# Two windowed attention layers: values with the tokens on the partitions, sums from a column of ones, and x normalised on ScalarE

## The reference

```
x = x + L0(gn(x))   # attention in 4 windows of 8x8 tokens, 12 heads of 8 channels, a bias per head
x = x + L1(gn(x))   # the same windows on the image rolled by 4, 12 heads of 32 channels, masks, a shared bias
x = x + L2(gn(x))   # depthwise 3x3 and pointwise convolution, quantised weights
x = x + L3(gn(x))   # linear attention with rounding
```

```
attn = softmax(q @ k.T * scale + bias)   # 64 x 64
out  = attn @ v                          # 64 x 8 (L0) or 64 x 32 (L1)
y    = concat(out over the heads) @ w_out + b
```

## Time and profile before

| | us |
|---|---|
| median of 3 runs | 624.99 |
| lowest, highest | 619.41, 633.68 |
| profiled execution, its own time | 622.26 |
| its span, first to last instruction | 620.5 |
| mean granted TensorE clock in it, share of full speed | 0.936 |
| busy: PE, VectorE, ScalarE, GpSimd | 448.3, 480.5, 236.2, 192.9 |

### The profile page before, as it was taken

The page is one execution under the profiler, slowest core; times in us unless marked ns, Lnnn a source line. Parts: engine busy times, 40 slices in busy tenths (PEclk is TensorE's granted clock), DMA queues, the critical chain, the costliest instruction groups (busy, mean ns, idle before and its releaser), DMA issues.

```text
span 620.5 us, 14087 instructions
## 1 busy us (share of the span) xinstructions
PE 448.3 (72%) x4973; PEld 291.5 (47%) x4973; DVE 480.5 (77%) x931; ACT 236.2 (38%) x538; POOL 192.9 (31%) x302
## 2 busy tenths in 40 slices
PE   0285787878787776877777777777776668856674
PEld 0284555656565554555555555555554322223342
DVE  0855798888888765788888888888887469957784
ACT  0001444444453333344444444444432123235763
POOL 6020444434343422322222222222233114330312
PEclk9999999999998788899999999999999789977887
DMA  9300000000000000000000000000000000000011
GB/s 278 53 2 0 3 3 2 0 0 0 0 0 0 1 1 1 2 1 1 1 0 0 0 0 0 0 0 0 0 1 2 1 0 1 0 2 13 13 39 39
DMA packets 8511, 7.08 MB, mean 11 GB/s; under 512 B 5058, under 2 KB 8130, under 8 KB 8354
## 3 DMA queue, kind: packets, MB, share of 16 engines
q1 hardware_dynamic: 3984, 5.26, 2.9%
q10 hardware_dynamic: 4498, 1.44, 1.3%
HBM read 5.13 MB, written 1.57 MB: 11 GB/s over the span
## 4 chain that ended last, share of the span: by engine, by line
PE 49%; DVE 32%; issue 8%; ACT 6%; DMA 2%; POOL 1%; DVEq 1%; ACTq 1%; POOLq 0%
DVE inv_sum L942 13%; PE bank L757 9%; PE bank L727 9%; PE bank L766 6%; PE bank L779 5%; PE bank L816 4%; DVE conv L1177 4%; PE bank L784 3%; PE bank L1258 3%; PE bank L794 3%; DVE v L885 3%; DVE probs L927 2%; DMA table<-in_L_conv_rpb_table 2%; PE bank L560 2%; PE bank L800 2%
## 5 line engine op out<-in xcount | busy, mean ns | idle before, releaser
L967 POOL TENSOR_TENSOR probs<-probs,row_max 128x384 f32<-128x384 f32 x128 | 106.5, 832 | 292.7 <-DVE row_max L929 292.7
L942 DVE RECIPROCAL inv_sum<-bank 128x384 f32<-128x384 f32 (+1 forms) x48 | 109.8, 2287 | 30.2 <-PE bank L784 21.8
L825 ACT ACTIVATE probsT<-bank 128x384 f32<-128x384 f32 x128 | 62.8, 491 | 158.5 <-PE bank L766 158.3
L927 DVE TENSOR_TENSOR probs<-bank,bias 128x384 f32<-128x384 f32 x128 | 70.4, 550 | 39.0 <-PE bank L757 37.9
L929 DVE TENSOR_REDUCE row_max<-probs 128x6 f32<-128x384 f32 x128 | 70.8, 553 | 4.4
L766 PE MATMUL bank<-cst,probs 128*128 128x128 f32 x384 | 71.7, 298 | 0.8 <-ACT probsT L825 0.7
L727 PE MATMUL bank<-xn,w 128*128 128x256 f32 x192 | 51.4, 406 | 26.8 <-ACT k L861 22.5
L757 PE MATMUL bank<-k,q 64*64 64x128 f32 x1536 | 62.0, 295 | 8.8 <-DVE probs L927 5.8
L757 PEld LDWEIGHTS bank<-k,q 64*64 64x64 f32 x1536 | 46.0, 143 | 30.8 <-issue 29.5
L766 PEld LDWEIGHTS bank<-cst,probs 128*128 128x128 f32 x384 | 45.6, 147 | 27.4 <-issue 18.1
L727 PEld LDWEIGHTS bank<-xn,w 128*128 128x128 f32 x192 | 35.0, 195 | 43.6 <-ACT k L861 26.4
(11 more groups left out here) (146 smaller groups left out, 688.1 us busy)
## 6 DMA issues: line engine op xcount, KB each, us to landing
rel_bc<-in_L_conv_rel_index SPq DMA_DIRECT2D x1, 2048.0 KB, 8.9
x<-in_x SPq DMA_DIRECT2D x4, 384.0 KB, 12.1
out_dram<-y_out SPq DMA_DIRECT2D x8, 192.0 KB, 2.1
cst<-in_consts ACTq DMA_DIRECT2D x1, 485.0 KB
w<-in_L_conv_w_qkv ACTq DMA_DIRECT2D x1, 432.0 KB, 4.7
p<-in_L_conv_w_out ACTq DMA_DIRECT2D x1, 144.0 KB, 4.6
pos<-in_L_conv_pos_emb SPq DMA_DIRECT2D x8, 2.0 KB
b_qk<-in_L_conv_qkv_b ACTq DMA_DIRECT2D x8, 0.1 KB, 6.7
```

The costliest lines, as they stand in the source:

```text
L825: nc.scalar.activation(probsT[w][:, :], ps_probsT[:, 0:NP * 128], ACT.Exp).then_inc(L.s.probsT_sb, 1)
L927: nc.vector.tensor_tensor(out, scores, b, ALU.add).then_inc(L.s.biased, 1)
L942: nc.vector.reciprocal(of(inv), of(ps_sums)).then_inc(L.s.inverted, 1)
L967: nc.gpsimd.tensor_tensor(probs[w][:, :, :], probs[w][:, :, :], by_row(row_max[w]), ALU.subtract).then_inc(L.s.shifted, 1)
```

## The change

- `pe_values`: `probsT` is now the stationary operand (64 columns) and v the moving one. v has a column of ones behind the channels of each head, so that a product of 66 columns in L1 (18 in L0) gives values and sums for two heads at once. The tokens lie on the partitions. Products 784 and 800 are gone; there are still 12 products per pair.
- `dve_heads`: the reciprocal of 12 sums per partition (L1, per pair) or 24 (L0, per sample), and one product with it repeated over the channels (128x384 or 128x192), into the new `headsN`.
- `pe_turn` (new): TensorE transposes that back, 3 transposes per pair in L1, 2 per sample in L0; `act_heads` (new) copies it out of PSUM into the buffer that the output product reads.
- `act_norm` in place of `dve_norm`: x is normalised by ScalarE as rstd*x + shift.
- The second v of L1 is copied out by VectorE, no longer by ScalarE.
- The output product `pe_out(s-1)` moves from before scores(s+1,0) to after q (L0) or qk0, qk1 (L1) of s+2; `act_out(s-1)` moves from w = 1 to the end of w = 3, behind the copies there.
- The bias of v is added in `act_heads`, product 552 and its wait are gone: the bias table's products wait for their one-hot input alone. Eight small memsets of ones and a shorter table of constants.

The diff, cut:

```
...
-        v0 = [sb(f"v0_{i}", [128, NW * NP, NU, NU * NH * HD0]) for i in range(2)]
+        v0 = [sb(f"v0_{i}", [128, 2, 2 * NP * NU, NH * (HD0 + 1)]) for i in range(2)]
-        v1 = [sb(f"v1_{i}", [128, NW, NP * NU, NH * HD1]) for i in range(2)]
+        v1 = [sb(f"v1_{i}", [128, NW, NP * NU, NH * (HD1 + 1)]) for i in range(2)]
-        inv_sum = [sb(f"inv_sum{i}", [128, NP * PAIR_COLS]) for i in range(2)]
+        inv_sum = [sb(f"inv_sum{i}", [128, 2 * HEADS]) for i in range(2)]
+        headsN = [sb(f"headsN{i}", [128, INNER]) for i in range(2)]
...
-            dve.wait_ge(pe_prep, PE_BV)
-            step(nc.vector.tensor_tensor(p0_bv[:, :], bank[1][0:C, C:C + 1], p0_b[:, :], ALU.add))
...
-            pe.wait_ge(dve_prep, done["p0T"])
-            nc.tensor.matmul(bank[1][0:C, C:C + 1], p0T[0:C, :], b0_v[:, :], start=True, stop=True).then_inc(pe_prep, 1)
+            pe.wait_ge(dve_prep, done["onehot"])
...
-                        ("v", 0, "dve", 4), ("v", 1, "act", 4)]
+                        ("v", 0, "dve", 4), ("v", 1, "dve", 4)]
...
+            for g in range(NP * NU):
+                p, u = g // NU, g % NU
                 for c in range(2):
...
+                    last = nc.tensor.matmul(ps_heads[c * WT:(c + 1) * WT, at_:at_ + n],
+                                            probsT[2 * j + u][:, p * 128 + c * WT:p * 128 + (c + 1) * WT], v,
+                                            start=True, stop=True)
...
+        def pe_turn(pe, L, s, j):
+
+            pe.wait_ge(L.s.divided, head_count(L, s, j))
+            wait(pe, L.s.heads_sb, heads_before(L, s, j, 1))
+            rows = 128 if L.wide else C
+            for p in range(NP if L.wide else 2):
+                last = nc.tensor.transpose(ps_headsT[0:rows, p * 128:(p + 1) * 128],
+                                           head_buffer(L, s, j)[:, p * rows:(p + 1) * rows], ident)
+            last.then_inc(L.s.turned, 1)
...
+        def act_norm(act, L, s):
...
+            for of_image, of_tokens in window_pieces(L):
+                tokens = xn[parity(s)][0:C, :, :].rearrange("c w t -> c (w t)")
+                nc.scalar.activation(of_tokens(tokens), of_image(image(x_of(s))), ACT.Identity, bias=gn_shift[:, bass.ds(s * 1, 1)],
+                                     scale=gn_rstd[:, bass.ds(s * 1, 1)]).then_inc(L.s.xn_ready, 1)
...
+        def act_heads(act, L, s, j):
+            act.wait_ge(L.s.turned, head_count(L, s, j))
...
+                nc.scalar.copy(heads1[parity(s)][:, :, j * PAIR_COLS:(j + 1) * PAIR_COLS],
+                               ps_headsT[:, 0:NP * PAIR_COLS].rearrange("r (p q) -> r p q", p=NP)).then_inc(L.s.heads_sb, 1)
...
+                nc.scalar.activation(heads0[parity(s)][0:C, :], ps_headsT[0:C, 0:T], ACT.Identity,
+                                     bias=b0_v[:, 0:1]).then_inc(L.s.heads_sb, 1)
...
+            nc.vector.reciprocal(inv, src[:, :, L.hd]).then_inc(L.s.inverted, 1)
+            dve.wait_ge(L.s.inverted, head_count(L, s, j))
+            nc.vector.tensor_tensor(dst, src[:, :, 0:L.hd], inv.unsqueeze(2).broadcast_to([128, groups, L.hd]),
+                                    ALU.mult).then_inc(L.s.divided, 1)
...
                     if q[2]:
                         pe_qkv(pe, L, *q)
-                if j == 0 and prev:
-                    pe_out(pe, L, moved(s, -1))
+                    if w == 2 and prev:
+                        pe_out(pe, L, moved(s, -1))
+                if (j and L.wide) or (not j and prev):
+                    pe_turn(pe, L, *pair_at(s, j - 1))
 
         def act_sample(act, L, s, prev, nxt, nxt2):
             for w in range(NW):
+                if w == 2 and prev:
+                    act_heads(act, L, moved(s, -1), 1)
+                if w == 0 and L.wide and prev:
+                    act_heads(act, L, moved(s, -1), 0)
                 act_exp(act, L, s, w)
                 evacuate_step(act, "act", L, s, w, nxt, nxt2)
-                if w == 1 and prev:
+                if w == 1 and nxt2:
+                    act_norm(act, L, moved(s, 2))
+                if w == 3 and prev:
                     act_out(act, L, moved(s, -1))
...
-                if w == 1 and nxt2:
-                    dve_norm(dve, L, moved(s, 2))
...
+            act_norm(act, L, 0)
             evacuate_first(act, "act", L, 0, 0, L.qk_uses)
+            if before:
+                act_heads(act, before, B - 1, 1)
+            act_norm(act, L, 1)
             if before:
                 act_out(act, before, B - 1)
...
```

More of the change, by code:

```diff
@@ L71, in constants @@
     ch = np.arange(C)
[L72 to L75, removed]
     put("group_mean", (ch[:, None] // GROUP == ch[None] // GROUP) / np.float32(GROUP * T), C)
@@ L156, in build @@
         ps_probsT = bank[2]
-        ps_sums = bank[3]
+        ps_headsT = bank[3]
         ps_heads = bank[4]
@@ L403, in build @@
                         *(t[:, :, :, :] for t in pad)]
+        one_columns = [(t, h, hd) for t, hd in (*((t, HD0) for t in v0), *((t, HD1) for t in v1)) for h in range(NH)]
+        ZEROED = len(zero_buffers) + len(one_columns)
         def pool_prepare(pool):
@@ L408, in pool_prepare @@
                 pool.wait_ge(zeroed, i + 1)
+            for i, (t, h, hd) in enumerate(one_columns):
+                nc.gpsimd.memset(t[h * WT:(h + 1) * WT, :, :, h * (hd + 1) + hd], 1.0).then_inc(zeroed, 1)
         def pool_prepare_late(pool):
@@ L771, in pe_values @@
             pe.wait_ge(L.s.probsT_sb, win_count(s, 2 * j + 1))
-            par = parity(s)
+            par, n = parity(s), NH * (L.hd + 1)
             if L.wide:
                 evacuated(pe, L, s, L.qk_uses + j)
[L775 to L789, removed]
-                for c in range(2):
[L791 to L803, removed]
@@ L806, in pe_out @@
         def pe_out(pe, L, s):
-            pe.wait_ge(L.s.heads_sb, pair_count(s, 1) if L.wide else s + 1)
+            pe.wait_ge(L.s.heads_sb, head_count(L, s, 1))
             wait(pe, L.s.y_ready, s * 1)
@@ L831, in act_out @@
             nc.scalar.activation(y_attn[:, :], ps_mix[0:C, 0:T], ACT.Identity,
-                                 bias=(p1_b if L.wide else p0_bv)[:, 0:1]).then_inc(L.s.y_ready, 1)
+                                 bias=(p1_b if L.wide else p0_b)[:, 0:1]).then_inc(L.s.y_ready, 1)
         def evac_q(eng, L, s, i, j, slot):
@@ L949, in dve_new_x @@
             dve_stats(dve, L.n + 1, s)
-        def dve_norm(dve, L, s):
-            if isinstance(s, int) and s < 2 and L.n:
-                dve.wait_ge(L0.s.v_ready, (B - 1 + s) * L0.v_uses)
-            wait(dve, L.s.v_ready, s * L.v_uses - L.v_uses)
-            for of_image, of_tokens in window_pieces(L):
-                tokens = xn[parity(s)][0:C, :, :].rearrange("c w t -> c (w t)")
-                nc.vector.tensor_scalar(of_tokens(tokens), of_image(image(x_of(s))), gn_mean[:, bass.ds(s * 1, 1)],
-                                        gn_rstd[:, bass.ds(s * 1, 1)], ALU.subtract, ALU.mult).then_inc(L.s.xn_ready, 1)
         def by_row(r):
@@ L1079, in pe_first @@
             if before:
+                pe_turn(pe, before, B - 1, 1)
                 pe_out(pe, before, B - 1)
@@ L1446, in _ @@
             pe_last_values(pe, L1)
+            pe_turn(pe, L1, B - 1, 1)
             pe_out(pe, L1, B - 1)
@@ L1462, in _ @@
             act.wait_ge(late_in, LATE_IN)
-            act.wait_ge(dve_prep, done["p0_bv"])
             act_first(act, L0, None)
@@ L1467, in _ @@
             attention_loop(act, L1, act_sample, None)
+            act_heads(act, L1, B - 1, 0)
+            act_heads(act, L1, B - 1, 1)
             act_out(act, L1, B - 1)
```

61 lines of the change are left out of this document (32 added, 29 removed).

## The result

| | before | after |
|---|---|---|
| median of 4 runs, us | 624.24 | 590.27 |
| lowest, highest | 619.41, 633.68 | 587.53, 594.22 |
| profiled execution, its own time | 622.26 | 589.08 |
| its span | 620.5 | 587.1 |
| granted clock in it, share of full speed | 0.936 | 0.921 |

The ratio is 0.9485 [0.9395, 0.9575]: 5% faster, within 2.3 us of the forecast 588.

A forecast was written before the change was run, and what follows sets the result against it. VectorE and TensorE taking turns in a chain through the reciprocal was taken as the bound. Terms -4.9 - 0.7 - 14.7 - 3.5 - 3 - 9.5 = -36.3 took 622.26 to 586.0, 588 against run medians; range 571 to 608.

The forecast's parts named there:

- L0's loop (term -14.7): L0's period per sample falls from 9.85 to 8.8 us, over 14 samples -14.7 us.
- the GpSimd chain: In L0, y out, residual add, subtraction, second add, statistics and bias step set the period of 8.8 us.
- TensorE's floor: L0's period through TensorE's own loop of multiply and bias step, should GpSimd's path be quicker: 8.1 to 8.3 us.
- rival (d): Granted clock falls where TensorE waits in L1: +73 us there, 660 in all, slower than before; chance 0.04.
- L1's loop (-3): L1's period goes from 15.5 to 15.2 us; over 14 samples -3 us, bounds +7 and -11.
- the gain of the short reciprocal is given to two waits: In each L1 sample TensorE waits twice for 1.6 us, on VectorE's copy of v and ScalarE's of k.
- Seam (-3.5): Between L0 and L1, one shorter chain against the second v and a turn: -3.5 us, bounds -1 and -6.
- end of L1 (-9.5): From scores(15,1) to the first pad, three chains with shorter reciprocal and sums: -9.5 us, bounds -6 and -13.
- Preparation (-4.9 and -0.7): Before L0, bias products start earlier, moving all behind by 4.9 us; first normalisations on ScalarE give 0.7 more.
- the sign to look for: The first q product of L0 starts near 47.9 us, where it was 52.7.
- Rival (b): Loads and products of `pe_values` don't overlap, a pair takes 1.7 us: +24 us, 612 in all; chance 0.06.
- Small terms: Reciprocals of 12 and 24 sums cost 231 and 306 ns; ScalarE's normalisation pieces 0.33 to 0.5 us each.

The follow-up runs named there:

- y_first_L0: The changed kernel with ScalarE in L0 copying the output of s-1 out ahead of the three copies of q: 568.66 us, ratio 0.9188 to the kernel before.
- filler_L0: The changed kernel with six unread products of constants per L0 sample, where TensorE waits ahead of T(s,1): 574.67 us, ratio 0.9185 to the kernel before.
- v1_on_scalar: The changed kernel with the second v of L1 copied out by ScalarE again: 558.07 us, ratio 0.8951 to the kernel before.
- prep_alone: The kernel before with only the preparation changed, bias products waiting only for their one-hot input: 620.36 us, ratio 0.9979 to the kernel before.
- norm_on_vector: The changed kernel with x normalised on VectorE again: 629.63 us, ratio 1.0002 to the kernel before.
- norm_vector_filled: norm_on_vector with eight unread products per L1 sample ahead of qk1, where TensorE waited: 604.17 us, no ratio given.

## Why the prediction was right, and where it was not

- **The total**: 588 forecast, 590.27 measured. Against the profiled spans the sum said -36.3, and -33.4 came. But it came right by errors of opposite sign: L0's loop gave 12 us less than forecast for its 12 samples, and the seam and the end of L1 some 12 more. That these cancel was luck.
- **L0's loop (term -14.7)**: failed. Measured over 12 samples: -0.56. The walk itself held: period 8.8 forecast, 8.40 to 8.94 in the samples at full clock, with the GpSimd chain as the bound, which y_first_L0 took away. TensorE's floor without it was given as 8.1 to 8.3; it is 7.87. What failed was to price the granted clock in L1 alone, as rival (d), and to take L0's 7.3 us of TensorE work in a period of 8.8 at full clock. The walk made two new waits of TensorE there, 1.19 and 0.46 us, and every second sample behind them fell to the lower level, which cost 3 us each time. filler_L0 isolates it. The 9.85 to compare with was too short also: it is one sample, and the mean of the 12 before was 10.06.
- **L1's loop (-3)**: the period at full clock was 15.0 to 15.1 against 15.2 forecast, with the two waits on VectorE's v and on the copy of k, 1.7 and 1.58. Three of the 11 samples took 16.7 behind the wait for v, and the mean is 15.49, as before. (15.2 against 15.5 over 14 samples is -4.2, not the -3 of the sum.) The mechanism of rival (d) is there, with some 5 us in place of its 73.
- **The reading behind L1**: "the gain of the short reciprocal is given to two waits" is right, and v1_on_scalar shows that one line undoes one of them, for 32 us.
- **Seam (-3.5) and end of L1 (-9.5)**: too small. From L0's 13th reciprocal to L1's 4th the gain was 10.1, of which the L0 term had counted two samples, some 2 us. From L1's 26th reciprocal to the first pad it was 18.1 (16.97 and 6.42 to 5.28 us at the last), where the prediction counted from scores(15,1) on and got 9.5 for what measures 11.45. The last samples have no next one to fill them, and their work is a chain as the end is; the prediction gave them the loop's 0.25. And it priced the low clock there, 0.88 and 0.86 before, only for the products of the sums, while the whole stretches rose to 0.96 and 1.00; how much of the gain is which was not tested.
- **Preparation (-4.9 and -0.7)**: -4.66 to the first q product, at 48.08 against 47.9. The two terms add up to 5.6, which would have been 47.1, so the sum and the sign to look for didn't agree. prep_alone gives 3.99 for the first, 0.9 too little; the rest, 0.67, is near the second.
- **`pe_values`**: 0.85 us for 24 records in L1's chain and 0.88 in L0's timeline, forecast 0.85 and 0.8. Rival (b), loads that are not overlapped, isn't there. The Trainium skill's page TensorE: Matmul & The Clock Gate, section LDWEIGHTS (loading the stationary operand), gives a load as columns/1.2 ns; an estimate from it for 24 loads of 64 columns is 1.28 us, and the trace, with 0.85 and 0.88, again disagrees.
- **Small terms**: the reciprocals at 228 and 307 ns, from 156 + 6.24 per element, are exact to 3 ns. ScalarE's pieces came at 0.40 to 0.48 us.
- **What didn't hold on the way**: the gain does not come from where VectorE's busy time fell. norm_on_vector has the short reciprocal too and is no faster than before.

The places where the clock fell are read from one execution of the kernel after. Its other three had a granted clock of 0.907, 0.915 and 0.932 over the whole span where this one has 0.921, so the loss is in all four; in which samples it lay there was not traced.

## What to carry to other kernels

When an edit frees an engine, look at what stands behind each job before giving it new ones: here the same change is worth 5% with the second v copied by VectorE and 10.5% with it copied by ScalarE, because TensorE's next product waited for that copy. Walk a period on one instruction that recurs, and subtract neighbours in the trace: stages that mix a loop and its ends hid that both loops had gained next to nothing. Price the granted clock wherever a walk leaves TensorE a new wait in each period, and if the wait can't go, try products in it whose result nobody reads.

## What the hardware showed that was not expected

- In L0, TensorE's granted clock fell behind two waits of 1.19 and 0.46 us with 1.2 us of work between them, in every second sample. Before, with waits of other lengths, the same stage mostly kept the full clock (0.94), and three of the 12 loop samples fell. The windows from 80 to 100 us, after and then filler_L0, where products fill the longer wait:

```profile
80.00:100.00 20.00, 17.20 (x240) 13.33 (x239) 12.72 (x30) 11.23 (x26) 8.22 (x12) 0.84 0.01 2
```

```profile
80.00:100.00 20.00, 19.50 (x304) 16.30 (x301) 14.50 (x34) 13.48 (x32) 9.28 (x14) 1.00 0.01 2
```

- Products that compute nothing made two kernels faster, the one with the fill in L0 by 16 us and the one with it in L1 by 17 to 25 us.
- The same waits do not always bring the fall: in L1 after, 1.70 to 1.79 us before qk1 left eight samples of eleven at full clock, and in L0's last loop samples the waits stayed and the clock was full. And the unfilled L0 of norm_vector_filled kept a clock of 1.00 with waits of 0.72 to 0.88 and 0.38 to 0.45, where norm_on_vector, with the same code there, fell in two samples. What decides between them stays open.
